# Moving the expansion of the image three ahead in front of the opening matmul and the mix in TensorE's round

## What is computed

```python
x = x + L0(_gn(x))      # a gate per image and channel, from channel means through two small spline layers
x = x + L1(_gn(x))      # the block below; nearly all the time goes here

# L1: routes are softmaxes over 4 filters, from two small convolution branches and pixel means
xp = star_scale * square(relu(einsum('bhwc,mc->bhwm', x, w_pw1))) + star_bias     # 128 -> 256 channels
xf = rfft2(xp);  weight = einsum('bfc,hwf->bhwc', routeing, complex_weights)
xs = irfft2(xf * weight)
out = einsum('bhwm,dm->bhwd', xp * einsum('bfc,hwf->bhwc', spatial_routeing, spatial_weights) + xs, w_pw2)
```

## Time and profile before

| what | value |
|---|---|
| median of 3 executions | 252.99 us (252.12 to 253.65) |
| the profiled execution | 253.25 us |
| span of its profile | 251.5 us |
| TensorE matmuls busy | 230.1 us (91%) |
| VectorE busy | 205.1 us (82%) |
| ScalarE busy | 145.4 us (58%) |
| GpSimd busy | 121.3 us (48%) |

### The profile page before, as it was taken

How to read it: one execution, slowest core, us unless ns; L and a number is a source line. 1 busy time by engine, 2 the same in 40 slices (tenths; PEclk the granted TensorE clock), 3 DMA queues, 4 the chain that set the end, 5 groups by cost and what they waited for, 6 DMA issues and landing times. The chain is left out here.

```text
span 251.5 us, 6954 instructions
## 1 busy us (share of the span) xinstructions
PE 230.1 (91%) x2257; PEld 180.4 (72%) x2257; DVE 205.1 (82%) x549; ACT 145.4 (58%) x348; POOL 121.3 (48%) x205
## 2 busy tenths in 40 slices
PE   0597799999999998999999999979999999999993
PEld 0587765545545554787869887968989898999992
DVE  3988999973958722799948999989898999989882
ACT  2034486744974756465636666656666575766641
POOL 2432450220000012457646676667686878778771
PEclk9999999999999999799999999999999999999999
DMA  7999300000000000000000100100101010101011
GB/s 211 371 325 329 152 0 3 1 4 0 3 3 0 3 0 0 1 4 25 21 21 23 42 25 21 44 22 23 42 21 42 21 42 21 42 21 41 24 42 64
DMA packets 9483, 13.19 MB, mean 52 GB/s; under 512 B 732, under 2 KB 8924, under 8 KB 9332
## 3 DMA queue, kind: packets, MB, share of 16 engines
q1 hardware_dynamic: 9428, 12.80, 15.6%
q10 hardware_dynamic: 32, 0.08, 0.2%
HBM read 8.69 MB, written 4.19 MB: 51 GB/s over the span
## 5 line engine op out<-in xcount | busy, mean ns | idle before, releaser
L431 POOL TENSOR_TENSOR eo<-xp 128x256 f32<-128x256 f32 x32 | 23.3, 729 | 72.2 <-ACT xp L608 72.0
L1338 PE MATMUL bank<-later_sb,qt_eo 128*128 128x128 f32 x256 | 36.0, 285 | 3.2 <-DVE bank L1045 1.6
L1216 PE MATMUL bank<-z_all,split_h 128*64 128x450 f16 (+2 forms) x320 | 37.4, 374 | 1.0 <-ACT z_all L518 1.0
L1338 PEld LDWEIGHTS bank<-later_sb,qt_eo 128*128 128x128 f32 x256 | 31.9, 196 | 5.4 <-DVE bank L1045 3.5
L1390 PE MATMUL bank<-later_sb,prod 128*128 128x128 f32 x256 | 34.0, 276 | 0.4 <-DVE prod L1055 0.4
L1328 PE MATMUL bank<-later_sb,eo 128*128 128x128 f32 x256 | 34.3, 277 | 0.0
L615 ACT ACTIVATE w_slot<-bank 128x512 f32<-128x512 f32 x32 | 19.1, 598 | 24.9 <-PE bank L1362 24.9
L1390 PEld LDWEIGHTS bank<-later_sb,prod 128*128 128x128 f32 x256 | 31.1, 192 | 1.1 <-DVE prod L1055 0.6
L1328 PEld LDWEIGHTS bank<-later_sb,eo 128*128 128x128 f32 x256 | 31.6, 194 | 0.4 <-issue 0.4
L437 POOL TENSOR_TENSOR qt_eo<-qt 128x256 f32<-128x256 f32 x32 | 27.5, 861 | 7.3 <-PE bank L1338 5.3
L438 POOL TENSOR_TENSOR qt_eo<-qt 128x256 f32<-128x256 f32 x32 | 28.8, 900 | 0.0
(11 more groups left out here) (181 smaller groups left out, 468.9 us busy)
## 6 DMA issues: line engine op xcount, KB each, us to landing
x_all<-in_x SPq DMA_DIRECT2D x8, 512.0 KB, 8.7
out<-x_all SPq DMA_DIRECT2D x32, 128.0 KB, 1.7
sp_t<-in_branch_s SPq DMA_DIRECT2D x1, 2560.0 KB, 15.4
later_sb<-in_later SPq DMA_DIRECT2D x1, 918.5 KB, 8.8
sym_all<-in_sym SPq DMA_DIRECT2D x1, 292.5 KB
early_sb<-in_early SPq DMA_DIRECT2D x1, 278.0 KB, 3.5
rwf_t<-in_branch_r SPq DMA_DIRECT2D x1, 256.0 KB, 11.8
kan_sb<-in_kan ACTq DMA_DIRECT2D x1, 80.8 KB, 3.2
```

The lines of the kernel that those rows point to most:

```text
L431: pool.tensor_tensor(eo[p][:, 1, :], xp[p][:, 0, :], xp[p][:, 1, :], ALU.subtract).then_inc(odd_ready, 1)
L1216: last = mm(dst[:, :, rows_out, cols_out], w[:, t, :], pixels(z_all[:, b:b + 2, part, :])[:, :, rows_in, cols_in], start=(n == 0 and t in ...
L1338: last = mm(total[:, m, :, 64 * odd:64 * odd + 64], qt_eo[:, odd, m * P:(m + 1) * P], forward[:, odd, :, :], start=False, stop=(odd == 1 a ...
```

## The change

In `round_of` of TensorE one line moves up by four: `expand(i + 3)` is issued directly behind `waves_of(i + 1)`, ahead of `prime`, `mix` and `turn_route`. Nothing is added or removed, no wait changes, and the other engines' lists stay as they are. The written-out rounds 28 to 31 keep their old order.

```diff
                 waves_of(i + 1, 1 - j)
+                expand(i + 3)
                 prime(i + 1, rows_of(1 - j, 0))
                 mix(i + 2, pair + 1, j)
                 if j:
                     turn_route(pair + 2, half)
-                expand(i + 3)
                 if isinstance(i, int) and i == 0:
                     pe.wait_ge(s1_ready, 2 * NIT)
                 reduce(i)
```

## The result

The changed kernel takes 260.9 us in the median against 253.75 beside it: a ratio of 1.0284, with a 95% interval from 1.0251 to 1.0317, about 7.2 us. I had forecast 257.3 and a range up to 259.4. The direction was right, and the time went to the two paths that I had added up. But I held ScalarE's path to decide in every round, and it decides in odd rounds only; in even rounds VectorE's path does. The size was too small on both.

A forecast was written before the change was run, and what follows sets the result against it. TensorE's own pace was taken to bound the loop rounds. Seven pairs at 0.53 us more (3.7) plus 0.6 for rounds 0 to 13 gave 4.3 us, a median of 257.3 us, range 254.6 to 259.4.

The forecast's parts named there:

- ScalarE's path: Loop rounds, mix through ScalarE's copy of y to compose's load: decides, load 2.24 (even) and 2.49 us (odd) after the opening.
- VectorE's path: Loop rounds, opening matmul through VectorE's multiplications to compose's load: 2.11 to 2.36 us after the opening, taken as 2.22.
- What bounds the kernel before: Loop rounds 14 to 27: TensorE runs at its own pace, never held, 8.60 us per pair; nothing to gain.
- TensorE's own path: Loop rounds if nothing else is late: 4.32 and 4.44 us, a pair 8.76, 0.16 more than now.
- closing stretch: From compose's first weight load to the next opening, with the six matmuls added: 2.21 us after even openings, 2.19 after odd.
- sign of being wrong: Named refutations: loop pair under 8.8 us, waits at L1338 instead, or longer VectorE or GpSimd rows.
- Rounds 0 to 13: Rounds before the loop: delays in rounds 6, 8, 12 and 13 only, together 0.6 us (0.3 to 0.8).
- the 0.66 fit in: Early rounds where VectorE sets the pace: terms starts 1.2 us or more after the opening, absorbing the 0.66 us delay.
- rival (c): VectorE's adds and GpSimd's overlap differently in half of the 14 rounds: 3.3 us on top, 260.6 us; chance 0.12.
- (a): ScalarE's path has unseen slack; only TensorE's exit cost is left, 1.1 us, 254.1 us; chance 0.09.
- (b): Faster: reduce hides the exit from the 32-row matmuls, saving up to 1.4 us, 251.6 us; chance 0.04.
- (d): The move does nothing, since TensorE's queue starts what is ready first: 253.0 us; chance 0.03.

The follow-up runs named there:

- the control: The kernel before with the loops of TensorE, ScalarE and VectorE written out: ratio 0.9989 (0.9957 to 1.002), 8.60 us per loop pair.
- the written-out loops: The changed kernel with the loops of TensorE, VectorE and ScalarE written out, so waits are on constants: ratio 1.0167 (1.0106 to 1.0229), a pair 8.99 us.
- TensorE's own cost: Changed kernel, loops written out, VectorE's first multiplication halved: 257.4 us, a pair 8.78; with ScalarE's copy of y also ahead of the rectification: 262.8 us, 8.77.
- the half move: The kernel before with three of the six expansion matmuls moved ahead of the opening, three left behind the mix: ratio 1.0043 (1.0013 to 1.0073), a pair 8.73 us.

## Why the prediction was right and wrong

**What bounds the kernel before**: right but for 0.03 us. Nothing was gained, and the control shows that faster waits bring that kernel next to nothing. But the slack that I saw was not there. These lines of the odd loop round stand in the trace of the kernel before:

```profile
206.46 0.97 PEld L1338 LDWEIGHTS bank<-later_sb,qt_eo 128*128 128x128 f32 x8
...
206.77 0.38 ACT L628 ACTIVATE y_sb<-bank 128x256 f32<-128x256 f32 x1 [0.15 <-PE bank L1390]
```

L628 ends at 207.15. TensorE would be ready at 206.46 + 0.89 = 207.35 and loads at 207.38, as late in every odd loop round; in the control the load comes without these 0.03. So that wait binds already, 0.23 us behind the end of the copy. The 0.2 us of slack that I read in the even round, from 202.77 to 202.97, was this release and no slack.

**TensorE's own path**: right, 8.76 forecast, 8.73 measured where neither path holds it. The closing stretch was forecast as 2.21 and 2.19; measured 2.19 and 2.20 (211.90 to 214.09, 207.31 to 209.51).

The sentence that no change in the number of drains means no cost is not borne out: the number of entries into and exits from the 32-row matmuls stayed the same, and the pair cost 0.13 more, because the expansion no longer makes up part of an exit. The rule of the Trainium skill (TensorEngine Tiling (Array Packing), Tiling Modes) that a change of the tiling mode drains TensorE agrees with the 0.21 us for which the weight loads are idle on each side of the 32-row matmuls; the price of the move does not follow from it.

**ScalarE's path**: the mechanism and its sum to the end of the copy were right: 2.13 and 2.38 after the opening forecast, 2.13 and 2.37 measured. The step that failed is the term behind it, from the end of the copy to the weight load. I bounded it by 0.05 and 0.16 and took 0.11; it is 0.22. With 0.22 the odd round is 2.37 + 0.22 + 2.19 = 4.78 for the 4.79 measured. The 0.16 was no upper bound: it is what a loop round shows more than a written-out one, and the 0.05 is the whole release in a written-out round. Their sum is 0.21, near the 0.22 measured. (For VectorE's release the same sum would be too much: it is 0.13.)

**VectorE's path**: I put it just short of ScalarE's in even rounds, with L1044 at 0.53 after the opening and 0.05 to the load. It is 0.61 and 0.13, and so this path decides the even rounds, against my forecast: 0.61 + 0.76 + 0.13 + 0.89 + 2.19 = 4.58 for the 4.59 measured, where 4.45 was forecast. TensorE is held there 0.29 us at L1338, which I had named as a sign of being wrong. The start was inside my bounds (0.42 to 0.67), but I chose the middle without a reason. The nearest row, ScalarE released by the same group of matmuls after 0.67, was the better guide.

These three terms give 0.25 us per pair (9.38 for 9.13), 1.8 us in all.

**Rounds 0 to 13**: 1.7 us instead of 0.6. Rounds 6 and 8 each lost 0.28, not 0.15, by the same late start of L1044 (4.49 is VectorE's path with short release, as in the written-out loops), and round 13 0.24, not 0.1. I had not counted the 0.4 at the lower clock ahead of round 0. And in round 9, in which VectorE sets the pace, the step that failed is "the 0.66 fit in": the opening did come in time, but VectorE's own work grew. The timeline of the changed kernel:

```profile
154.87 0.73 POOL L437 TENSOR_TENSOR qt_eo<-qt 128x256 f32<-128x256 f32 x1
...
154.91 0.97 DVE L1025 SCALAR_TENSOR_TENSOR eo<-xp,shift 128x256 f32<-128x256 f32 x1
...
155.56 0.92 POOL L438 TENSOR_TENSOR qt_eo<-qt 128x256 f32<-128x256 f32 x1
```

and of the kernel before, in the same round:

```profile
148.72 0.73 POOL L431 TENSOR_TENSOR eo<-xp 128x256 f32<-128x256 f32 x1 [1.27 <-ACT xp L608]
...
149.31 0.48 DVE L1025 SCALAR_TENSOR_TENSOR eo<-xp,shift 128x256 f32<-128x256 f32 x1
...
149.40 0.97 POOL L437 TENSOR_TENSOR qt_eo<-qt 128x256 f32<-128x256 f32 x1
```

The even sum takes twice as long after the move. GpSimd is at work beside it in both timelines; what differs is how much is left of the GpSimd instruction that is running when L1025 starts. After the move L437 has just begun and ends at 155.60, and L1025 ends 0.28 us behind that. Before, L431 is nearly done (it ends at 149.45), L1025 takes 0.48, and it is the next GpSimd instruction, L437, that takes 0.97 for 0.73. The rule holds in all twelve profiles. Between 104 and 241 us L1025 starts 331 times beside a running GpSimd instruction, or at most 0.04 us ahead of one. In 330 of them it ends 0.28 us after that instruction's end, within 0.01, or takes 0.48 us where that is longer. (At 0.05 us ahead of one it goes either way.) So one of the two waits for the other, and which one is set by who comes first.

This is the mechanism of rival (c), in the place where VectorE has no slack. In the loop it is there as well (1.03 us in even and 0.62 in odd rounds, for 0.48). But L1044 waits for the opening in even rounds anyway, and with the three terms above nothing is left for it to explain. The longer rows of VectorE were the second of my signs of being wrong that came.

**The rivals**: (a), (b) and (d) fell, as TensorE's own cost, the written-out loops and the half move show. ScalarE started 0.65 to 0.67 after the opening, not before 0.45. The range fell short because both release terms were bounded by written-out rounds or by an increment taken for a whole, and because rounds 0 to 13 cost nearly three times what I gave them.

## What to carry to other kernels

When one engine is busy throughout, moving its steps can't gain time by releasing others earlier, but it can lose time by releasing them later: add up each path from the moved release back to the busy engine, and compare it with the slack that the trace shows. Count the time from a result to its waiter as a term of its own, and take it from a wait of the same kind in the same form of loop. A gap between a result and its use is slack only as far as it is longer than that term: look first whether the user starts later than its own work would let it. And ask of two engines that work on the same memory which instruction starts first, since a move can turn that round. Half of a move that costs much can cost almost nothing, since slack is used up first.

## What the runs showed of the hardware

- In a hardware loop, with waits on register values, TensorE is released 0.22 us after ScalarE's copy and 0.13 us after VectorE's multiplication; written out, with constants, 0.04 to 0.06 and 0.05. ScalarE starts 0.65 to 0.67 us after the opening in the loop, 0.51 written out. Whether it is the loop, the number of waits or their form, no run here tells.
- A busy share of 100% for TensorE's matmuls does not exclude such waits: in the written-out changed kernel it is 17.50 of 17.50 us (182 to 199.5 us), with TensorE held for 0.19 us in each even round.
- VectorE starts 0.59 to 0.61 us after the start of the 32-row, 512-column opening matmul whether or not the mix runs beside it, 0.2 us behind its modelled end of 0.38.
- The next weight load stands 0.33 us behind the opening of the 32-row matmuls whichever step follows. Six float16 expansion passes then make up 0.09 us of it, eight float32 passes nothing; the new order costs TensorE 0.13 us per pair of rounds.
- VectorE's even sum takes from 0.48 to 1.05 us. It ends 0.28 us behind the GpSimd instruction that was running when it started, or takes 0.48 where that is longer (330 of 331 cases).
